# A four-stage vision kernel: the place of GpSimd's input buffers shifted by 8 bytes, and a sixth state's input product moved from VectorE to GpSimd

## The reference

```python
def selective_scan(u, delta, A, B, C):
    def step(h, inp):
        u_, de_, b_, c_ = inp
        dA = jnp.exp(de_[..., None] * A)
        h = h * dA + (de_ * u_)[..., None] * b_[:, None, :]
        y = jnp.einsum('bdn,bn->bd', h, c_)
        return (h, y)
```

## Time and profile before

| | us |
|---|---|
| median of three runs | 768.14 |
| the three runs | 762.94, 768.14, 768.19 |
| span of the profiled execution, first to last instruction | 765.8 |
| the scan in it (first scan to last) | 301.4 to 615.0 |
| VectorE busy | 660.8 |
| TensorE busy (matmuls) | 626.2 |
| ScalarE busy | 502.1 |
| GpSimd busy | 453.1 |

### The profile page before, as it was taken

How to read it: one execution, slowest core, us unless ns; L and a number is a source line. 1 busy time by engine, 2 the same in 40 slices (tenths; PEclk the granted TensorE clock), 3 DMA queues, 4 the chain that set the end, 5 groups by cost and what they waited for, 6 DMA issues and landing times.

```text
span 765.8 us, 11653 instructions
## 1 busy us (share of the span) xinstructions
PE 626.2 (82%) x3947; PEld 359.6 (47%) x3947; DVE 660.8 (86%) x906; ACT 502.1 (66%) x598; POOL 453.1 (59%) x282
## 2 busy tenths in 40 slices
PE   7899999999989933677776778777767789799997
PEld 5655547667764310344453445444534553233332
DVE  7899996889967889999899999998999974788886
ACT  2657512789965868677876877777777710477673
POOL 3798983000001175999999999799899820532321
PEclk9999999999999975689988887899897999899999
DMA  2004100430001030000000000000000004100000
GB/s 56 5 13 103 27 1 12 80 96 8 3 3 58 24 93 17 1 1 0 1 1 0 1 0 1 0 1 1 0 2 0 1 20 80 42 1 1 14 1 14
DMA packets 28853, 14.98 MB, mean 20 GB/s; under 512 B 23022, under 2 KB 24942, under 8 KB 28654
## 3 DMA queue, kind: packets, MB, share of 16 engines
q1 hardware_dynamic: 27582, 13.61, 8.0%
q10 hardware_dynamic: 1216, 0.66, 0.4%
HBM read 5.14 MB, written 0.78 MB: 8 GB/s over the span
## 4 chain that ended last, share of the span: by engine, by line
PE 40%; DVE 37%; ACT 9%; issue 8%; POOL 4%; DVEq 0%; DMA 0%; SPq 0%; ACTq 0%; POOLq 0%
PE ps L572 38%; DVE arena L1380 14%; DVE ps L1053 8%; DVE arena L1053 4%; DVE arena L1099 4%; ACT arena L1620 3%; POOL arena L1781 3%; DVE ps L1099 2%; PE ps L754 1%; ACT arena L1734 1%; DVE arena L1267 1%; ACT x L1734 1%; DVE arena L1331 1%; PE ps L633 1%; ACT arena L1606 1%
## 5 line engine op out<-in xcount | busy, mean ns | idle before, releaser
L572 PE MATMUL ps<-arena 128*32 128x64 f32 (+5 forms) x2072 | 345.5, 357 | 110.7 <-DVE arena L1380 37.1
L572 PEld LDWEIGHTS ps<-arena 128*32 128x32 f32 (+4 forms) x2072 | 125.3, 124 | 245.9 <-issue 97.4
L1781 POOL TENSOR_TENSOR arena<-arena 128x1024 f32<-128x1024 f32 x81 | 188.3, 2337 | 25.6 <-DVE arena L1380 8.5
L1380 DVE TENSOR_TENSOR_SCAN arena<-arena,ps 128x1024 f32<-128x1024 f32 x66 | 150.9, 2287 | 9.0 <-ACT ps L1721 0.5
L1766 ACT ACTIVATE arena<-ps,nycol 128x1024 f32<-128x1024 f32 x64 | 71.1, 1115 | 57.6 <-PE ps L572 57.6
L1053 DVE TENSOR_TENSOR ps<-arena,ps 128x1024 f32<-128x1024 f32 x75 | 90.9, 1212 | 10.0 <-PE ps L572 9.2
L1721 ACT ACTIVATE arena<-arena,a_col 128x1024 f32<-128x1024 f32 x66 | 75.4, 1143 | 16.7 <-DVE arena L1380 16.0
L1902 POOL TENSOR_TENSOR arena<-arena,bmask 128x128 f32<-128x128 f32 x64 | 30.8, 482 | 78.8 <-PE ps L572 67.7
L1053 DVE TENSOR_TENSOR arena<-ps,arena 128x512 f32<-128x512 f32 (+2 forms) x75 | 48.6, 654 | 25.7 <-PE ps L572 20.1
L1380 DVE TENSOR_TENSOR_SCAN arena<-ps,arena 128x1024 f32<-128x1024 f32 x30 | 68.1, 2271 | 2.7 <-POOL arena L1781 2.7
L572 PE MATMUL ps<-ident,arena 128*128 128x128 f32 x416 | 65.9, 312 | 2.0 <-POOL arena L1781 2.0
(11 more groups left out here) (208 smaller groups left out, 1045.8 us busy)
## 6 DMA issues: line engine op xcount, KB each, us to landing
arena<-arena SPq DMA_DIRECT2D x54, 64.0 KB
arena<-arena SPq DMA_DIRECT2D x12, 128.0 KB, 3.3
w_conv<-in_c_far SPq DMA_DIRECT2D x1, 1152.0 KB, 5.7
w_conv<-rpb_pad SPq DMA_DIRECT2D x36, 28.0 KB, 1.8
arena<-x SPq DMA_DIRECT2D x12, 64.0 KB, 2.0
arena<-x1t SPq DMA_DIRECT2D x12, 64.0 KB, 2.0
arena<-x3t SPq DMA_DIRECT2D x12, 64.0 KB, 2.0
arena<-arena SPq DMA_DIRECT2D x2, 288.8 KB, 3.7
```

What stands on the lines that cost most here:

```text
L572: return pe.matmul(o, l, r, start=start, stop=stop, **k)
L1380: ve.tensor_tensor_scan(hs_ring[n % RING], decay, add, 0.0, ALU.mult, ALU.add).then_inc(S("scan"), 1)
L1781: return gp.tensor_tensor(o, a, b, ALU.mult)
```

## The change

It has two parts. Buffers are shifted by `SKEW` = 2 floats, 8 bytes, in both stages, so that the two inputs of GpSimd's products no longer start at the same place of a 16-byte line; the arena grows by 16 floats. And `SHARED` has six states, not five, so that six input products of the 16 of a tile are on GpSimd.

```diff
+SKEW = 2
...
-SHARED = (3, 6, 9, 12, 15)
+SHARED = (3, 6, 8, 11, 13, 15)
...
-        ARENA = 39948
+        ARENA = 39964
...
         off_rep = cv(2, 2, NBLK, B * G, CG)
         hat_xm = cv(2, T)
         hat_yp = cv(2, T)
+        cv(SKEW)
         hat_ym = cv(2, T)
+        cv(SKEW)
         term = cv(2, 4, T)
         tmp_a = cv(T)
         tmp_b = cv(T)
         tmp_p = cv(T)
+        cv(SKEW)
         tmp_m = cv(2, T)
...
         zs = cv(PAIRS, T)
         u = cv(DIRS, PAIRS, T)
+        cv(SKEW)
         delta = cv(DP, T)
         du = cv(DP, T)
+        cv(SKEW)
         split_b = cv(DP, T, dt=BF16, rows=96)
...
         da = cv(2, T)
         dbu = cv(2, T)
+        cv(SKEW)
         hs = cv(2, T)
+        cv(SKEW)
         c_sb = cv(2, T)
         hc = cv(2, T)
         xs = cv(2, T + 2 * (KC - 1))
...
-        hs_ring = [hs[:, 0], hs[:, 1], xs[:, 0, 0:T], xs[:, 1, 0:T]]
+        hs_ring = [hs[:, 0], hs[:, 1], xs[:, 0, SKEW:SKEW + T], xs[:, 1, 0:T]]
         c_ring = [c_sb[:, 0], c_sb[:, 1], x1[:], x1t[:]]
         hc_ring = [hc[:, 0], hc[:, 1], x3t[:], xn[:]]
```

## The result

| | before | after |
|---|---|---|
| median of the runs, us | 766.71 (4 runs) | 747.52 (4 runs) |
| lowest and highest | 762.94, 768.19 | 747.03, 748.80 |
| profiled execution: its time, its span | span 765.8 | 747.03, span 745.2 |
| ratio of the times, 95% interval | | 0.9759 [0.973, 0.9788] |

The kernel is faster by 2.4%. A fourth run of before moved its median from 768.1 to 766.7; by the medians the gain is 19.2 us, by the spans 20.6.

The account below looks back on a forecast made before the run. VectorE was taken to bound the kernel, with GpSimd 4.5 us behind in the scan. Terms -7.9 - 2.7 - 0.7 - 1.2 + 3.0 = -9.5 us took the median of 768.1 to 758.6 us, range 750.5 to 769.

Parts of the forecast that it names:

- input product moved: Scan, VectorE: one input product less per tile saves 1.32 us, times six tiles, -7.9 us; bounds 0 and -7.9.
- GpSimd's wait: Scan: state 12's scan no longer starts 0.46 us late behind GpSimd in each tile, -2.7 us; bounds 0 and -2.7.
- start: Scan's start: VectorE's product du ends sooner as GpSimd's two products beside it shorten, -0.7 us; bounds 0 and -0.7.
- end: Scan's end: GpSimd's last four products, which TensorE's collection waits for, get shorter, -1.2 us; bounds 0 and -1.5.
- offset convolution: Offset convolution: GpSimd's products shorten by 6.5 us in all, hidden behind VectorE's chain, so 0.
- TensorE's order: Scan: b_share and b_rep queue behind copies and collections, adding waits at state 10, +3.0 us; bounds -3 and +18.
- the reading of eight bytes: GpSimd: products whose inputs lie 8 bytes apart in a 16-byte line are about 380 ns shorter, near 1.97 us.
- the 0.9 us to spare for state 14: Scan, TensorE: state 14's chain takes 7.0 us at full clock, needed after 7.9; at the lower clock nothing to spare.
- rival A: Scan: TensorE is late at state 14, about 3 us a tile, 18 in all, giving 773.6 us; chance 0.08.
- Rival C: Scan: states 5, 7, 10 and 14 give the product's time back in waits for TensorE, 763.5 us; chance 0.25.
- Rival B: GpSimd: the distance does nothing for most pairs, one 2.36 us product more per tile, +14.2 us, 782.3; chance 0.04.
- D: Scan: TensorE keeps pace, state 11's waits of about 3 us go and nothing comes, 752.6 us; chance 0.13.

Follow-up runs that it names:

- the heavy dummies: 8, 16 and 8 dummy matmuls per tile on TensorE in the scan, added to the kernel after (767.72 us) and to the distance alone (769.39 us).
- the light ones: Three and six zero-adding matmuls on TensorE in the scan, without a wait, added to the kernel after (747.50 us) and to the distance alone (759.67 us).
- the other six: The kernel after with shared states 3, 6, 9, 11, 13, 15 instead of 3, 6, 8, 11, 13, 15: 752.32 us.
- the two of the last stage: The kernel after with dummy matmuls ahead of the last stage's first samples: 751.58 us with the larger number, 748.27 us with the smaller.

## Why the prediction was right and wrong

| step | forecast, us | measured in the traces, us |
|---|---|---|
| input product moved | -7.9 | -7.9 |
| GpSimd's wait | -2.7 | -3.2 |
| start (measured: all up to the first scan) | -0.7 | -0.9 |
| end | -1.2 | -2.1 |
| offset convolution | 0 | -0.1, within the row above |
| TensorE's order (measured: what is left in the scan) | +3.0 | -4.1 |
| last stage | not named | -2.4 |
| sum | -9.5 | -20.6 |

**Right.** The product moved gave its 1.32 us in each tile, since VectorE was the bound and stayed it. GpSimd's products are at 1996 ns throughout, so the reading of eight bytes from x1t's pairs and from the image shifts held; the Trainium skill, GPSIMD Engine Reference, section on instruction dispatch, gives two inputs a floor of about 2.5 cycles an element and names no effect of their place, and these products, at 1996 ns, lie below the 2.13 us that the prediction estimated from it. The scans no longer wait for GpSimd. The waits for TensorE that are left stand ahead of states 5 and 10, with at most 0.2 us at 7 and none at 12 and 14, as the 0.9 us to spare for state 14 said: rival A did not come. Rival C did not either. Rival B's kernel, in effect, is the sixth state alone: 774.6 us, +7.9. Its price of 782.3 was too high by the prediction's own figures, which left GpSimd 4.3 us a tile (48.0 of 52.3) for a product of 2.36.

**Wrong: the term of +3.0 us for TensorE's order**, 7 of the 11 us missed. It was built by adding state 10's waits to state 5's at the clock of before, "half a microsecond a tile beyond today's". Measured are 4.1 us fewer. State by state after, beyond its own work, in the order of the tiles: state 5: 1.05, 0.01, 0.95, 0.23, 0.31, 0.23; state 10: 0.01, 0.36, 0.01, 0.92, 0.01, 0.95. Before, state 5 had 1.15, 1.68, 1.08, 0.82, 1.75, 1.03, and state 11 1.08, 0.23, 0.59, 1.09, 0.23, 0.01. So state 10 took 11's part, as forecast, and cost 2.3 us against 3.2. But state 5's cost fell from 7.5 us to 2.8, though its neighbours 3 to 6 are what they were. With the distance alone it was 3.9, and state 11's 5.0: the pair of tight places went from 10.7 us to 8.9 by the distance, and to 5.0 by the sixth state. The prediction took state 5's wait for a property of the order ("goes on paying"). The order around it is unchanged and the wait fell by more than half, so it is not; what it does depend on is taken up below.

One wait is new, 1.0 us for TensorE at the last product before the last scan (L929 in the waits above); the 4.1 us are net of it, and of some 0.6 us net in places under 0.4 each. TensorE's timeline in tile 2 of after, the place of the earlier trace rows:

```profile
409.14 1.89 PE L580 MATMUL ps<-arena 96*128 96x512 bf16 x4 [3.32 <-DVE arena L1388]
412.14 1.04 PE L580 MATMUL ps<-arena 96*128 96x512 bf16 x2 [1.12 <-ACT arena L1742]
412.97 1.91 PE L580 MATMUL ps<-ident,xn 128*128 128x128 f32 x8
414.68 1.35 PE L580 MATMUL ps<-arena 96*128 96x512 bf16 x4
415.87 1.04 PE L580 MATMUL ps<-ident,arena 128*128 128x128 f32 x8
```
```profile
415.64 1.23 DVE L1061 TENSOR_TENSOR ps<-arena,ps 128x1024 f32<-128x1024 f32 x1 [0.83 <-PE ps L580]
```
```profile
408.00:415.00 7.00, 4.75 (x15) 2.58 (x16) 6.67 (x4) 3.96 (x4) 4.54 (x3) 0.54 0.00 0
415.00:460.00 45.00, 30.32 (x190) 19.15 (x188) 43.17 (x24) 37.63 (x39) 41.44 (x22) 0.99 0.00 1
```

The pattern of before is there (an idle time of 3.32 us, a pair at 1.89 us, a collection at 1.91, state 5 late by 0.83), with a clock of 0.54. Then come 45 us at 0.99, almost a tile, in which VectorE does not wait for TensorE again. Within the scan of before 16 stretches at the 1.2 GHz level begin, within that of after seven.

The tie of wait and clock can be counted over all fourteen traces, at the two states of each tile where the order is tight. Looked at is the clock in the 6 us before the product was due, roughly the 5.73 us that the order leaves it. With under 1.5 us of them at the 1.2 GHz level, the mean wait was 0.16 us (78 places, six above 0.7 us); with 1.5 to 3.5 us, 0.51 (42 places); with more than 3.5, 0.90 (48 places, 33 above 0.7). That is a correlation. The runs that should have made it a proof are confounded (the heavy dummies) or did not move the clock (the light ones).

**Why the clock stays high with six is open.** It isn't the shorter products (the distance alone: 0.84) nor the sixth state alone (0.86). Among the kernels with six states less time at the low level goes with a shorter scan: 86.8 us of 315.5 without the distance, 77.6 of 309.2 at 12 bytes, 66.4 of 301.5 at 4, 60.9 of 300.9 with the other six, 49.9 of 298.4. But part of that row is chance, and the low level alone moves the scan little: three traces with after's very code in the scan (the distance in the scan only, and the two of the last stage) have 50.2, 60.7 and 64.5 us at the low level, in scans of 298.6, 299.1 and 299.4 us. So 14.6 us more at half clock went with 1.0 us more of scan. What else separates the kernels of the row is mostly scans that wait for GpSimd (14.9, 10.1 and 2.7 us in the first three). A circle in which a late TensorE makes VectorE late, which leaves TensorE idle again, would suit the row too; but TensorE's idle gaps of over 1 us sum to about as much after (69.7 us) as before (73.5), and no run broke the circle at one point. Which of the two drives the other was not shown.

**The last stage** was in no term: its code is untouched, and it gave 2.4 us. With the distance alone it lost 0.6. Over the kernels that leave this stage's code alone it took 112.9 to 116.2 us. A stage that follows can come out some 3 us longer or shorter; the range should have held that, on both sides. That the place of the low-clock stretch decides is argued, not shown.

**The end** was 0.9 us short: besides the four products, VectorE's last product beside them went from 1.75 to 1.23 us, and the prediction let VectorE's part count against the gain instead of for it.

**The rivals.** D (TensorE keeps pace, 752.6) was nearest and still 5 us high; its 0.13 was too little, and its floor set the range's end. It took away only state 11's waits, where the trace of before had 9.2 us of waits for TensorE in nine, of which up to 6 more could go. The bound of -3 on this term should have been near -9.

## What to carry to other kernels

When two inputs of a GpSimd product come from one array, look at how far apart they start within a 16-byte line and in which direction they run: here 8 bytes apart is 15% shorter than aligned, and it costs a few bytes. An engine at its limit is worth relieving first for what can then be moved onto it: the relief alone gave 6.7 us, the move alone cost 7.9, both gave 19.2. When a wait stands beside rows at half of TensorE's clock, don't forecast it as a constant of the order: bound it from nothing to all of today's waits, and give each later stage with a low-clock stretch a few us both ways, since here 112.9 to 116.2 us were measured for one and the same code.

## What the runs showed of the hardware

- GpSimd's product of 128x1024 float32 takes 2.34 to 2.37 us or 1.94 to 2.01 us (means of each kind of pair and direction in before, after and the kernels at 12 and 4 bytes) by where its inputs stand within 16 bytes, and which distances are short depends on the direction (4 and 8 forward, 8 and 12 backward).
- VectorE's product of two SBUF inputs that starts while a product of GpSimd runs ends 1.08 us after GpSimd's (1.078 to 1.085), however much of GpSimd's was left: so in all 18 cases in the fourteen traces, at the scan's start and end, with lengths from 1.74 to 2.65 us. At the start it went from 2.65 to 1.93 us because GpSimd's ended sooner; at the end it went from 1.75 to 1.23 because it no longer overlaps (GpSimd ended at 598.08 us, it began at 598.97). The Trainium skill, SBUF — State Buffer, section on its two separate sides, says that a VectorE operation with two inputs in SBUF and a GpSimd operation that reads SBUF lock each other out for a whole instruction. The traces agree.
- The time at the 1.2 GHz level in one stretch of nearly the same work ranged from 49.9 us (after) to 102.0 (before), and with the very same code in the stretch from 49.9 to 64.5.
- Raising the clock from 0.92 to 0.95 with dummy matmuls cost 20.2 us (medians 747.5 to 767.7). A float32 matmul of a 128x128 identity shows as two of 0.13 us at full clock; 8 of them took 2.05 us and 16 took 3.84 in tile 2.
